# Recommendation tower on one core: layer 0's rotated rows taken from shifted product tiles, gathers issued in spaced bursts, layer 0 of pairs 1 and 2 moved inside the slots

## What is computed

```python
x0 = e; xk = e
for W in (W0, W1, W2):                 # W0: (32, 32, 64); W1, W2: (32, 64, 64)
    xk = relu(einsum('bmd,bhd,mhk->bkd', x0, xk, W))
    outs.append(sum(xk, axis=2))
h = concat([concat(outs, axis=1), dense_ctx], axis=1)    # (1024, 208)
h = relu(h @ W_top1 + b_top1); h = relu(h @ W_top2 + b_top2)
y = h @ W_top3                         # (1024, 1)
```

## Time and profile before

| | us |
|---|---|
| median of 3 runs | 660.87 (660.35 to 661.81) |
| the profiled execution, its own time | 659.91 |
| its span in the profile | 658.1 |
| TensorE busy | 602.4 (92%) |
| VectorE busy | 528.1 (80%) |
| GpSimd busy | 453.6 (69%) |
| ScalarE busy | 391.4 (59%) |

### The profile page before, as it was taken

One profiled execution on the slowest core, in us unless ns is written; L12 is line 12 of the kernel. 1 busy time (PEld: TensorE's weight loads), 2 busy tenths in 40 slices (PEclk: granted clock), 3 DMA queues, 4 the chain that ended last, 5 costly groups with the idle time before them and its releaser, 6 DMA issues.

```text
span 658.1 us, 7277 instructions
## 1 busy us (share of the span) xinstructions
PE 602.4 (92%) x2634; PEld 192.6 (29%) x2634; DVE 528.1 (80%) x281; ACT 391.4 (59%) x631; POOL 453.6 (69%) x306
## 2 busy tenths in 40 slices
PE   1765497789999999999999999999999999999998
PEld 1211122223333333333333333333333333333343
DVE  1065198499989898999999898989898999899700
ACT  0200254386767676767677776858586867677231
POOL 5367365488989788878788878888598855267300
PEclk9997698989999999999999999999999999999999
DMA  4193969594959595968778695949494939450000
GB/s 134 40 226 71 238 168 248 155 236 112 249 129 238 118 249 127 233 148 211 162 204 177 186 198 162 219 146 218 136 222 113 246 92 248 109 97 0 9 8 1
DMA packets 38413, 103.44 MB, mean 157 GB/s; under 512 B 13764, under 2 KB 22856, under 8 KB 30184
## 3 DMA queue, kind: packets, MB, share of 16 engines
q1 hardware_dynamic: 28900, 98.72, 60.8%
q0 software_dynamic: 8192, 2.11, 3.4%
q10 hardware_dynamic: 1284, 2.13, 1.0%
HBM read 97.69 MB, written 4.20 MB: 155 GB/s over the span
## 4 chain that ended last, share of the span: by engine, by line
PE 84%; another core or an unknown queue 5%; issue 4%; ACT 2%; POOL 2%; ACTq 1%; DVE 1%; DMA 1%; SPq 0%; DVEq 0%; POOLq 0%
PE acc L660 65%; PE pair_sum L596 8%; PE pair_sum L576 5%; POOL gath L325 2%; PE pair_sum L640 2%; PE rep L746 2%; PE rep L738 1%; PE rep L739 1%; ACT rep L480 1%; DVE prod L399 1%; ACTq L445 1%; DMA gath<-in_tables,rows_sb 0%; ACT prod_pool L501 0%; SPq L245 0%
## 5 line engine op out<-in xcount | busy, mean ns | idle before, releaser
L399 DVE TENSOR_TENSOR prod<-m_rep,rep 128x2048 f32<-128x2048 f32 x223 | 494.5, 2281 | 56.3 <-DMA m_rep<-x_scratch 28.5
L660 PE MATMUL acc<-prod,w_sb 128*64 128x512 f32 x1792 | 406.0, 602 | 18.3 <-DVE prod L399 13.7
L480 ACT COPY rep<-state 32x512 f32<-32x512 f32 x488 | 283.4, 581 | 59.3 <-DVE prod L399 43.3
L325 POOL DMA_INDIRECT gath<-in_tables,rows_sb x256 | 243.1, 949 | 101.5 <-issue 75.2
L660 PEld LDWEIGHTS acc<-prod,w_sb 128*64 128x64 f32 x1792 | 124.9, 138 | 290.9 <-issue 274.4
L336 POOL TENSOR_TENSOR prod_pool<-m_rep,xb 128x2048 f32<-128x2048 f32 x32 | 146.3, 4571 | 51.7 <-PE acc L660 26.1
L336 POOL TENSOR_TENSOR prod_pool<-x_rot,x_rep 128x2048 f32<-128x2048 f32 x14 | 64.1, 4578 | 9.4 <-DMA x_rot<-x_scratch 9.2
L660 PE MATMUL acc<-prod_pool,w_sb 128*64 128x512 f32 x256 | 60.4, 592 | 0.0
L473 ACT ACTIVATE sums_sq<-pair_sum 128x1024 f32<-128x1024 f32 x30 | 30.8, 1027 | 45.5 <-PE pair_sum L576 25.4
L452 ACT ACTIVATE state<-pair_sum 128x512 f32<-128x512 f32 x16 | 9.6, 597 | 74.2 <-PE pair_sum L640 58.9
L576 PE MATMUL pair_sum<-x0c,sel_sb 32*128 32x512 f32 x120 | 35.7, 672 | 13.8 <-issue 9.5
(11 more groups left out here) (52 smaller groups left out, 102.9 us busy)
## 6 DMA issues: line engine op xcount, KB each, us to landing
m_rep<-x_scratch SPq DMA_DIRECT2D x64, 1024.0 KB
x_rot<-x_scratch SPq DMA_DIRECT2D x30, 512.0 KB
x_rep<-x_scratch SPq DMA_DIRECT2D x15, 512.0 KB
gath<-in_tables,rows_sb POOLq DMA_INDIRECT x256
x_scratch<-gath SPq DMA_DIRECT2D x31, 128.0 KB
x0c<-x_scratch SPq DMA_DIRECT2D x26, 64.0 KB
w_sb<-in_w ACTq DMA_DIRECT2D x2, 512.0 KB
m_rep<-z_sb SPq DMA_DIRECT2D x12, 64.0 KB, 2.3
```

The costliest lines, as they stand in the source:

```text
L325: pool.indirect_dma_start(out=gath[p % 2][:, g, :], out_offset=None, in_=tables, in_offset=bass.IndirectOffsetOnAxis(ap=rows_sb[:, n:n + 1 ...
L399: nc.vector.tensor_tensor(prod[:, number % RING], in0, in1[:, None, :].to_broadcast([128, 2, PAIR]), ALU.mult).then_inc(unit_ready, 1)
L480: last = nc.scalar.copy(rep[v][M * q:M * q + M, CHUNK * a:CHUNK * a + CHUNK], state[l - 1][K * a + M * v:K * a + M * v + M, :])
L660: last = nc.tensor.matmul(acc[K * a:K * a + K, :], w, src[:, k, CHUNK * a:CHUNK * a + CHUNK], start=start and k == 0, stop=stop and k == 1)
```

## The change

- `x_rot` and its two transfers for each pair are gone. The rows of an `m_rep` tile are placed anew: partition n of tile t holds row n//4 + n%4 + t (before: 2(n//8) + t). Tiles 1 and 5 are then the rotated rows, and `layer0_product` reads them. The weights are permuted to match (`by_tile`).
- `layer0_product(p)` now waits for `x_rep` and for `m_rep` transfers j = 0 and j = 2 of the same pair. The four transfers are issued in the order 0, 2, 1, 3.
- GpSimd issues gathers 16 to 63 in bursts of four. Between bursts from gather 20 on stands a product of 128 x 256 elements that nothing reads (`unread`). The waits on VectorE's products are gone. `ahead` starts at 64.
- The products of pairs 1 and 2 are both VectorE's, in slot 1 behind its second unit and in slot 2 behind its fourth. Pair sums and layer 0 of pairs 1 and 2 move on TensorE into slots 1 and 2. ScalarE takes the relu of slot 0 ahead of pair 1's squares. In slot 3 the pair sums stand behind units 2 and 4 instead of 0 and 3.

```diff
-POOL_SEQ = [("x", 2)]
+POOL_SEQ = []
+        def x_loaded(eng, p):
+            m_loaded(eng, p, 0)
+            m_loaded(eng, p, Q // 2)
+            eng.wait_ge(x_in, 16 * (p - EARLY + 1))
+        def x_rot(p):
+            first = p % M_BUFS * T + 1
+            return m_rep[:, first:first + Q + 1:Q, :]
...
                     sp.dma_start(x_rep[:, :], src).then_inc(x_in, 16)
-                    for t in range(XT):
-                        row = x0_dram[p, 1 + Q * t:2 + Q * t, :]
-                        src = bass.AP(row.tensor, row.offset, [[PAIR, M], [PAIR, Q], [1, PAIR]])
-                        sp.dma_start(x_rot[:, t, :], src).then_inc(x_in, 16)
                 if p >= M_BUFS:
                     slot_read(sp, SLOT_OF[(2, p - M_BUFS)])
-                for j in range(T // 2):
+                for j in (0, 2, 1, 3):
                     row = x0_dram[p, 2 * j:2 * j + 1, :]
-                    src = bass.AP(row.tensor, row.offset, [[2 * PAIR, 128 // T], [0, T], [1, 2 * PAIR]])
+                    src = bass.AP(row.tensor, row.offset, [[PAIR, M], [PAIR, Q], [1, 2 * PAIR]])
...
             gather(0, FIRST_RUN)
+            pool.wait_ge(first_sq, 1)
+            gather(FIRST_RUN, BURST)
             pool.wait_ge(l0_done, 1)
-            gather(FIRST_RUN, 2 * GPP - FIRST_RUN)
-            for n in range(7):
-                pool.wait_ge(unit_ready, 2 * n + 1)
-                gather(2 * GPP + 4 * n, 4)
-            layer0_product(2)
-            for n in range(7, 10):
-                pool.wait_ge(unit_ready, 2 * n + 1)
-                gather(2 * GPP + 4 * n, 4)
-            ahead = 72
+            pool.wait_ge(w1_in, 16)
+            ahead = 4 * GPP
+            for k, n in enumerate(range(FIRST_RUN + BURST, ahead, BURST)):
+                gather(n, BURST)
+                after(pool, burst_out, k)
+                nc.gpsimd.tensor_tensor(unread[:, :, :], w_sb[1][:, 0, 0:T // 2, :], w_sb[1][:, 1, 0:T // 2, :],
+                                        ALU.mult).then_inc(burst_out, 1)
...
+                    if (i, n) in ((1, 1), (2, 3)):
+                        layer0_product(i)
...
             relu0(0)
+            relu_slot(0)
             square_x(1)
             square(1, 0)
+            replicate(1, 1)
             square(1, 1)
-            relu_slot(0)
-            replicate(1, 1)
             relu0(1)
...
-                    if i == 0 and n in (5, 6):
-                        pair_sums(1, n - 5)
                     if (i, n) == (0, 7):
                         copy_state(1, 0)
-                        layer0_sums(1)
-                        layer0_rest(1)
-                    if (i, n) == (1, 7):
-                        pair_sums(2, 0)
-                    if (i, n) == (2, 1):
-                        pair_sums(2, 1)
-                    if (i, n) == (2, 2):
-                        layer0_sums(2)
-                    if (i, n) == (2, 3):
-                        layer0_rest(2)
+                        pair_sums(1, 0)
+                    if (i, n) == (1, 0):
+                        pair_sums(1, 1)
+                    if i == 2 and n in (1, 2):
+                        pair_sums(2, n - 1)
+                    if (i, n) in ((1, 2), (2, 3)):
+                        layer0_sums(i)
+                    if (i, n) in ((1, 3), (2, 4)):
+                        layer0_rest(i)
```

More of the change, by code:

```diff
@@ L32 @@
 FIRST_RUN = 16
+BURST = 4
 WARM_FROM = 10
@@ L65, in sums_to, with sums_at @@
     return QB * (p - 1)
-SUMS_AT = (0, 3)
+def sums_at(i):
+    return (2, 4) if i == POOL_FROM else (0, 3)
 def order(i):
@@ L114, in build @@
         x_rep = sb("x_rep", [128, PAIR])
-        x_rot = sb("x_rot", [128, XT, PAIR])
         xsq = sb("xsq", [128, CHUNK])
@@ L134, in build @@
         prod_pool = sb("prod_pool", [128, POOL_RING, 2, PAIR])
+        unread = sb("unread", [128, T // 2, K])
         early_sb = xb[0][:, 0:(XT + ST) * 128]
@@ L188, in build @@
         diag_half = sem("diag_half")
-        second_x = sem("second_x")
+        early_x = sem("early_x")
         xsq_ready = sem("xsq_ready")
@@ L202, in build @@
         z_in = [sem(f"z_in{i}") for i in range(2)]
+        burst_out = sem("burst_out")
         top_ready = sem("top_ready")
@@ L217, in m_loaded @@
             eng.wait_ge(m_in[p % M_BUFS][j], 16 * (p // M_BUFS + 1))
+        def x_loaded(eng, p):
[5 more added lines that the diff above has]
+            return m_rep[:, first:first + Q + 1:Q, :]
         def x_multiplied(eng, p):
-            if p == 1:
-                eng.wait_ge(second_x, 1)
+            if p <= 2:
+                eng.wait_ge(early_x, p)
             else:
@@ L332, in product @@
                 if at < POOL_RING:
-                    pool.wait_ge(l0_done, at + 1)
+                    pool.wait_ge(l0_done, at + 2)
                 else:
@@ L339, in layer0_product @@
             def layer0_product(p):
-                pool.wait_ge(x_in, 16 * (1 + XT) * (p - EARLY + 1))
-                product(POOL_AT[("x", p)], x_rot[:, :, :], x_rep)
+                x_loaded(pool, p)
+                product(POOL_AT[("x", p)], x_rot(p), x_rep)
             def units(i):
@@ L410, in sum_d, with layer0_product @@
                                         op=ALU.add, axis=AX_X).then_inc(z_ready[l], 1)
+            def layer0_product(p):
+                x_loaded(dve, p)
+                nc.vector.tensor_tensor(prod_pool[:, p - 1], x_rot(p), x_rep[:, None, :].to_broadcast([128, XT, PAIR]),
+                                        ALU.mult).then_inc(early_x, 1)
             for i, (l, p) in enumerate(SLOTS):
                 base, nv = UNIT_BASE[i], v0_units(i)
[L414 to L418, removed]
                 if i >= POOL_FROM:
@@ L632, in layer0_rest @@
                 x_multiplied(pe, p)
-                at = 1 if p == 1 else POOL_AT[("x", p)] % POOL_RING
+                at = p - 1 if p <= 2 else POOL_AT[("x", p)] % POOL_RING
                 for t in range(XT):
                     last = layer0_tile(w0_sb[:, t, :], prod_pool[:, at, t, :], False, False)
-                if p > 1:
+                if p > 2:
                     last.then_inc(pool_used, 1)
@@ L706, in _ @@
                         pool_unit(0)
-                    if i >= 3 and l == 1 and p + 1 < NP and n in SUMS_AT:
-                        pair_sums(p + 1, SUMS_AT.index(n))
-                    if i == 0 and n in (5, 6):
-                        pair_sums(1, n - 5)
+                    if i >= 3 and l == 1 and p + 1 < NP and n in sums_at(i):
+                        pair_sums(p + 1, sums_at(i).index(n))
                     if (i, n) == (0, 7):
                         copy_state(1, 0)
-                        layer0_sums(1)
-                        layer0_rest(1)
-                    if (i, n) == (1, 7):
-                        pair_sums(2, 0)
-                    if (i, n) == (2, 1):
-                        pair_sums(2, 1)
-                    if (i, n) == (2, 2):
-                        layer0_sums(2)
-                    if (i, n) == (2, 3):
-                        layer0_rest(2)
+                        pair_sums(1, 0)
[7 more added lines that the diff above has]
+                        layer0_rest(i)
                 if pooled:
@@ L789, in by_tile @@
         n, v, t = np.ix_(np.arange(128), np.arange(2), np.arange(T))
-        return np.asarray(w).reshape(M, 2 * M, K)[(2 * (n // T) + t) % M, M * v + n % M]
+        return np.asarray(w).reshape(M, 2 * M, K)[(n // Q + n % Q + t) % M, M * v + n % M]
     def by_column(v, n):
```

## The result

The changed kernel takes **730.58 us** (median of 4 runs, 728.58 to 736.2) where the kernel before, beside it, takes 660.61 us (658.72 to 661.81). The ratio is 1.1076, 95% interval [1.1009, 1.1142]. The profiled execution took 728.58 us, its span is 726.8.

What follows compares the result with a forecast made beforehand. TensorE's own work, 34.47 us per pair, bound the kernel. Fill gain, eleven loops of 45.2 us, then chain, product and last matmuls reach 678.5; 87.8 and 1.8 more give 768 us, range 720 to 815.

Steps and rivals of the forecast that it cites:

- the prediction's own case: Whole kernel: GpSimd's wait repeats in every pair; 768 us, own range 750 to 790, 55 in 100.
- a faster chain: Rival on the transfers: at 250 GB/s they take 12.9 us, time 752; a loop 4 us shorter gives 720; 10 in 100.
- The loop: Pattern of slots: layer 0's product waits, delaying the next pair's gathers and data; 45.2 us per pair, 10.7 over TensorE's 34.47.
- GpSimd's 23.9: GpSimd's work from layer 0's product until the next pair's last gather is issued: 13.2 plus 10.7 us.
- the landing 1.4: Chain's first part, from the end of a pair's last gather until its data have landed, on idle queues: 1.4 us.
- the stores 4.8: Chain's second part, the stores of the gathered data and their landing, on idle queues: put at 4.9 us.
- `x_rep` and two `m_rep` transfers, 2.5 MB: Chain's last part, ahead of layer 0's product: first MB 7.1 us, 1.5 more at 221 GB/s 7.1, together 14.2.
- The rule set against the rows: Transfer rate by the Trainium skill, 341 GB/s: 7.7 us for 2.62 MB, loop 38.7, time 690; the trace's row was preferred.
- some 5 us later: Slot 0: VectorE's third product waits for a transfer now arriving third, so the slot ends at 63.1 instead of 57.64.
- The fill: First slots: slot 1 starts at 67, slot 2 at 91, slot 3 at 118 instead of 131.87; gain 14 us.
- the signals freed by the bursts: First slots: spaced gather bursts let TensorE's signals come on time, ending ScalarE's waits of 18.1 us in two and 11.9.
- The sum: Pair 4's last gather ends at 152.6, eleven loops add 497.2; layer 0 of pair 15 ends at 678.5, then 87.8.

Runs made afterwards that it cites:

- e1: Changed kernel with 80 gathers ahead of slot 3 instead of 64, nothing else; 645.41 us, ratio 0.9864.
- e2: Kernel before with 64 gathers ahead of slot 3 instead of 72, its own tiles and placing kept; 727.3 us, ratio 1.1109.
- e4: Kernel before with only the new row placing in `m_rep` and the permuted weights, `x_rot` still loaded, 72 gathers ahead; 641.35 us, ratio 0.9804.
- e10: Kernel before with only the new row placing and permuted weights, run again on another chip; 642.22 us, ratio 0.9823.
- e8: Changed kernel with 80 gathers ahead of slot 3 and without the spacing products that nothing reads; 701.03 us, ratio 1.0515.
- e12: Changed kernel with 80 gathers ahead and no spacing products, the same program as e8 on another chip; 642.5 us, ratio 0.9818.
- e6: Changed kernel once more, no edit; 734.14 us, ratio 1.1032 to the kernel before.
- e7: Changed kernel with 68 gathers ahead of slot 3 instead of 64; 688.08 us (median of three runs), ratio 1.0312.

## Why the prediction was right, and where a term was off

- **How near it came.** The measured 730.6 us lies inside the stated range but under the 750 to 790 of the prediction's own case, to which it gave 55 in 100. That it is inside rests on the room left for "a faster chain" (10 in 100), not on the term that the forecast used. The direction and the loop were worked out; the size was not.
- **The loop.** Right. GpSimd's product waits for its own pair's data, its wait delays the gathers behind it, and with them the next pair's. e1 takes the loop away with the order alone, e2 makes it with the order alone. Of its terms GpSimd's 23.9, the landing 1.4, the stores 4.8 (forecast 4.9) and `x0c` 0.8 came as worked out. GpSimd's wait was 8.5 us in the mean (102.5 in twelve), where 11.7 was put.
- **The mis-sized term: "`x_rep` and two `m_rep` transfers, 2.5 MB", together 14.2.** It measured 41.47 - 23.9 - 7.0 = 10.6 us in the mean (9.2 to 11.8 in single turns). Its two rows, the first MB of pair 0 and the 221 GB/s of the earlier trace rows, were both of the old source pattern. The change itself had replaced it in the line of the diff that the prediction read as a placing of rows only, and e4 shows 420 GB/s by that line alone. The rival "a faster chain" had this direction at 12.9, with 250 GB/s.
- **The rule set against the rows.** By the 341 GB/s of the Trainium skill, "DMA: Bandwidth & Descriptors", Measured, the term was an estimated 7.7 us and the time 690. That table row's other figure, 6.15 us for 1 MB, would have given an estimated 15.4 us for 2.5 MB; the prediction used the rate alone. The trace agrees with neither: the queues reached 420 GB/s, yet the three transfers took 10.6 us. The measured time lies between the two that the prediction gave, 41 above the one and 37 under the other.
- **Slot 0, "some 5 us later".** It didn't come: VectorE ends slot 0 at 55.06, for the same cause; with faster transfers the order 0, 2, 1, 3 delays nothing. Slot 1 started at 59.30 instead of 67. The wait for `m_rep` in slot 1 came (5.88 us ahead of 69.67), slot 2 started at 89.42 (91) and slot 3 at 116.64 (118). The fill gains 15.2 where 14 were put; with slot 1 nearly 8 us early and slot 2 not 2, the agreement is in part luck. Half of the argument was wrong, too: I put the gain to the signals freed by the bursts. e10 has neither bursts nor moved layers, and gains 12.0 us over before with signals on time, by the transfers. The bursts count only where signals are late. By the times of before on two chips (660.6 and 654.5) the late signals are worth an estimated 6 of the 15.2 here. They are shorter than the earlier trace rows suggests: of the 11.9 us that the prediction read as a wait for a finished sum, only the last 4.9 lie behind the end of that sum (120.47 to 125.39). In the kernel after, 5.8 us of such waits are left, in two.
- **TensorE.** Busy 87%, not near 80%: the 602.4 us of before would be 83% of this span, and 27 us more are matmuls stretched by a lower clock, which count as busy (the 1792 of `acc<-prod` took 424.4 us instead of 406.0, the 120 of `pair_sum<-x0c` 43.0 instead of 35.7). In the window 201 to 205 us after, right behind the wait for `x0c`, the granted clock is 0.50, which is 1.2 GHz:

```profile
201.00:205.00 4.00, 3.50 (x8) 1.03 (x10) 0.00 (x0) 1.99 (x3) 0.96 (x2) 0.50 0.93 326
```

  The lower clock did not lengthen the loop, which runs over GpSimd, SyncE and the queues. The end goes over TensorE: behind the last wait for `x0c` (616.72) 22.3 us of its work follow without a gap, 24 matmuls of it at 7.84 us where the next 24 take 5.37, and layer 0 of pair 15 ends 31.5 us behind the pair's last gather (607.50), where 21.3 + 4.6 + 2.8 = 28.7 were put. The prediction had TensorE wait for the product only, not for `x0c`. It also read the clock's 6 tenths as the slice where TensorE was least busy; that is the fifth slice of the earlier trace rows, and the first, with 1 tenth busy, shows 9.
- **The sum.** Forecast 678.5 for layer 0 of pair 15, measured 639.0. The last gather of pair 4 came 2.5 earlier; eleven loops from gather to gather made (607.50 - 150.10) = 457.4 instead of 497.2, 39.8 less; the last stretch was 2.8 longer. 2.5 + 39.8 - 2.8 = 39.5. What follows took 726.8 - 639.0 = 87.8, as put.

## What to carry to other kernels

Where an engine both issues the loads of the next round and waits for the data of this one, count the instructions between the last load of a round and its first use, on that engine: if they are shorter than the way through memory, the wait feeds itself and its price is paid every round. Here that point made 83 us, and the whole rest of the change 15. And price a transfer with a row of the same source pattern: a diff that only permutes which row goes to which partition took the rate here from 221 to 420 GB/s.

## What the runs showed of the hardware

- **Source pattern.** `m_rep` with eight partitions reading the same 8 KB moved 221 GB/s at a DMA share of 1.05; with at most four on one start and starts a row apart it moved 420 at a share of 1.01 (e4). A row is still read by eight partitions, four of them as their first row and four as their second. Whether the shared starts or something else of the pattern makes the rate was not told apart.
- **Signals held back in gather runs.** In e8 ScalarE saw TensorE's finished sum 55 us late, behind a run of 60 indirect gathers without a break, and the same program on another chip showed no such lateness (e12). The kernel before took 661 and 665 us where its trace shows them late (by 12.0 us at the worst, 61.57 to 73.53 in the first trace). It took 654 on two other chips; it was not traced there, but none of the eight traces taken there has a wait of ScalarE without a releaser. With bursts of four and a product of 0.75 us between them, the relu of pair 1's layer 0 was 3.1 us late in e6 and 2.7 in e7, on the chip of e8. What on the chip makes the difference stays open.
